# Attention with the value matmuls in halves between the score halves, probability sums that alternate between two partial sums over the first eight key tiles, and denominators in four pieces instead of seven

## What is computed

```
q, k, v = x @ Wq.T, x @ Wk.T, x @ Wv.T            # split in 16 heads of 32
attn    = softmax(q @ k.T / sqrt(32))              # over 2048 keys, per head
x       = layernorm(x + attn @ v)
y       = (x @ sign(W).T) * scale + bias, clipped to +-100
out     = layernorm(x + y)
```

## Time and profile before

| what | value |
|---|---|
| median of 3 runs | 2724.6 us (2723.04 to 2725.27) |
| span of the profiled execution | 2721.4 us |
| around it: median less that span | 3.2 us (the execution's own time is not shown apart) |
| PE, ACT, DVE, POOL busy | 2686.9, 2261.1, 2308.4, 341.1 us |
| exponentials, first to last start | 549.9 to 2426.3 us |
| granted TensorE clock, mean | 0.994 |

### The profile page before, as it was taken

The page is one execution under the profiler, slowest core; times in us unless marked ns, Lnnn a source line. Parts: engine busy times, 40 slices in busy tenths (PEclk is TensorE's granted clock), DMA queues, the critical chain, the costliest instruction groups (busy, mean ns, idle before and its releaser), DMA issues.

```text
span 2721.4 us, 76294 instructions
## 1 busy us (share of the span) xinstructions
PE 2686.9 (99%) x32088; PEld 1351.0 (50%) x32088; DVE 2308.4 (85%) x1983; ACT 2261.1 (83%) x2726; POOL 341.1 (13%) x342
## 2 busy tenths in 40 slices
PE   9999999999999999999999999999999999979998
PEld 8888888733333333333333333333333333337887
DVE  7444444389999999999999999999999999978998
ACT  5333333399999999999999999999999999965665
POOL 1000000000000000010000000000000000005665
PEclk9999999999999999999999999999999999989999
DMA  6555555557686777768677686867768677655553
GB/s 227 191 194 193 188 186 186 197 132 169 132 176 140 155 157 158 162 126 184 138 153 165 142 172 135 167 147 157 168 131 172 141 159 158 150 145 177 189 189 136
DMA packets 216706, 445.22 MB, mean 164 GB/s; under 512 B 15570, under 2 KB 130258, under 8 KB 189780
## 3 DMA queue, kind: packets, MB, share of 16 engines
q0 software_dynamic: 27504, 200.29, 37.4%
q1 hardware_dynamic: 179108, 222.61, 26.2%
q10 hardware_dynamic: 9792, 17.83, 1.7%
HBM read 122.43 MB, written 117.96 MB: 88 GB/s over the span
## 4 chain that ended last, share of the span: by engine, by line
ACT 48%; PE 31%; issue 16%; DMA 3%; DVE 2%; SPq 0%; DVEq 0%; POOL 0%; ACTq 0%; POOLq 0%
ACT probs L769 48%; PE banks L226 19%; PE banks L1007 7%; DMA total<-partial 2%; PE banks L632 1%; PE banks L996 1%; PE banks L661 1%; PE banks L989 1%; PE banks L1003 1%; DVE partial L818 1%; DVE total L821 0%; DVE partial L821 0%; PE banks L248 0%; PE banks L990 0%; PE banks L254 0%
## 5 line engine op out<-in xcount | busy, mean ns | idle before, releaser
L769 ACT ACTIVATE probs<-banks 128x1024 f32<-128x1024 f32 x2048 | 1877.7, 1457 | 3.9 <-PE banks L632 3.9
L632 PE MATMUL banks<-score_rows 97*32 97x512 f16 x16384 | 1117.4, 380 | 4.5 <-issue 4.0
L661 PE MATMUL banks<-probs,v_keys 128*32 128x512 f32 x8192 | 1060.5, 592 | 0.1
L821 DVE TENSOR_TENSOR partial<-partial,probs 128x2048 f32<-128x2048 f32 x384 | 879.4, 2290 | 33.4
L632 PEld LDWEIGHTS banks<-score_rows 97*32 97x32 f16 x16384 | 361.3, 95 | 708.2 <-ACT probs L769 484.3
L818 DVE TENSOR_TENSOR partial<-probs 128x2048 f32<-128x2048 f32 x192 | 439.6, 2290 | 23.6 <-ACT probs L769 16.7
L601 POOL DMA_DIRECT2D total<-partial x191 | 164.7, 862 | 1713.7 <-DMA total<-partial 703.3
L661 PEld LDWEIGHTS banks<-probs,v_keys 128*32 128x32 f32 x8192 | 249.0, 111 | 209.9 <-ACT probs L769 0.2
L821 DVE TENSOR_TENSOR total<-total,probs 128x2048 f32<-128x2048 f32 x128 | 292.6, 2286 | 6.8
L354 DVE TENSOR_TENSOR qk_lo<-banks,qk_hi 128x512 f16<-128x512 f32 x128 | 88.3, 690 | 241.6 <-ACT qk_hi L309 241.6
L680 PEld LDWEIGHTS banks<-total,ones 128*32 128x32 f32 x3584 | 105.6, 109 | 280.7 <-issue 265.1
(11 more groups left out here) (95 smaller groups left out, 2117.5 us busy)
## 6 DMA issues: line engine op xcount, KB each, us to landing
total<-partial POOLq DMA_DIRECT2D x191, 1024.0 KB, 8.3
scratch_q_raw<-qk_raw SPq DMA_DIRECT2D x16, 1024.0 KB, 5.7
scratch_k_raw<-qk_raw SPq DMA_DIRECT2D x16, 1024.0 KB, 5.7
scratch_v<-v_out SPq DMA_DIRECT2D x16, 1024.0 KB, 5.1
score_rows<-scratch_q_hi SPq DMA_DIRECT2D x128, 128.0 KB, 4.6
score_rows<-scratch_k_hi SPq DMA_DIRECT2D x128, 128.0 KB, 3.5
v_keys<-scratch_v SPq DMA_DIRECT2D x64, 256.0 KB, 5.8
scratch_attn<-wf_scaled SPq DMA_DIRECT2D x64, 256.0 KB
```

Source lines behind the costliest of these rows:

```text
L632: last = nc.tensor.matmul(scores_of(phase, unit)[part, i, :], k_rows[:, h, keys], q_rows[:, h, qb * BLK:(qb + 1) * BLK], start=True, stop= ...
L661: last = nc.tensor.matmul(banks[rows, out_bank(qb), :], v_keys[:, kt, rows], probs[:, kt % P_RING, h, :], start=(kt == 0), stop=(kt == KT ...
L769: nc.scalar.activation(probs[:, kt % P_RING, heads, :], scores_of(it % SLOTS, qb * UNITS + u), ACT.Exp, scale=SCALE / GAIN ** 2).then_inc( ...
L821: nc.vector.tensor_tensor(into, into, probs[:, kt % P_RING], ALU.add).then_inc(a_sum, 1)
```

## The change

Three things are changed, all in `attend`.

1. The step of a key tile is cut in two on TensorE: first score half, first half of the values, second score half, second half of the values. A half of the values is columns 0 to 255 or 256 to 511 of the queries for all four heads, so each value matmul has 256 columns and there are twice as many. The waits of the values stand before the first half, the release of `a_pv` behind the second.
2. The sums take the tiles in another order of groups. Tiles 0 to 7 go alternately to group 0 and group 1 (`GROUP_OF = (0, 1) * PER + ...`), tiles 8 to 11 and 12 to 15 to groups 2 and 3 as before. The first add of group 0 is now that of tiles 0 and 2, the first of group 1 that of tiles 1 and 3. `TAKEN` counts for each tile how many tiles from the start are summed without a hole, and `a_sum` goes by it.
3. The denominators are cut in four pieces of 128 columns, behind tiles 8, 10, 12 and 14.

```diff
+GROUP_OF = (0, 1) * PER + (2,) * PER + (3,) * PER
+PREVIOUS = tuple(max((e for e in range(kt) if GROUP_OF[e] == GROUP_OF[kt]), default=None) for kt in range(KT))
+def taken_after(kt):
+    used = {e for k in range(kt + 1) if PREVIOUS[k] is not None for e in (PREVIOUS[k], k)}
+    return next(e for e in range(KT + 1) if e not in used)
+TAKEN = tuple(taken_after(kt) for kt in range(KT))
-DEN_TILES = tuple(range(8, 15))
-DEN_EDGES = (0, 80, 152, 224, 296, 368, 440, BLK)
+DEN_TILES = (8, 10, 12, 14)
+DEN_EDGES = (0, 128, 256, 384, BLK)
...
-        def values(it, qb, kt):
+        def values(it, qb, kt, part):
+            cols = slice(part * BLK // 2, (part + 1) * BLK // 2)
...
-                last = nc.tensor.matmul(banks[rows, out_bank(qb), :], v_keys[:, kt, rows], probs[:, kt % P_RING, h, :],
-                                        start=(kt == 0), stop=(kt == KT - 1))
-            last.then_inc(a_pv, 1)
+                last = nc.tensor.matmul(banks[rows, out_bank(qb), cols], v_keys[:, kt, rows], probs[:, kt % P_RING, h, cols],
+                                        start=(kt == 0 and part == 0), stop=(kt == KT - 1), skip_group_check=True)
+            if part == 1:
+                last.then_inc(a_pv, 1)
...
-                if kt + LAG < KT:
-                    scores(it, phase, qb, kt + LAG)
...
-                values(it, qb, kt)
+                for half in range(2):
+                    if kt + LAG < KT:
+                        scores(it, phase, qb, kt + LAG, (half,))
...
+                    values(it, qb, kt, half)
...
-                    g, place = divmod(kt, PER)
-                    if place == 0:
+                    g, before = GROUP_OF[kt], PREVIOUS[kt]
+                    if before is None:
                         continue
...
-                        nc.vector.tensor_tensor(into, probs[:, (kt - 1) % P_RING], probs[:, kt % P_RING], ALU.add).then_inc(a_sum, 2)
+                        nc.vector.tensor_tensor(into, probs[:, before % P_RING], probs[:, kt % P_RING],
+                                                ALU.add).then_inc(a_sum, TAKEN[kt] - TAKEN[kt - 1])
                     else:
-                        dve.wait_ge(a_sum, st * KT + kt + P_RING)
+                        dve.wait_ge(a_sum, st * KT + TAKEN[before] + P_RING)
```

More of the change, by code:

```diff
@@ L616, in _, with fast_scores @@
         pe.sem_inc(a_merged, GROUPS - 1)
-        def fast_scores(it, phase, qb, kt):
-            if kt == 0:
+        def fast_scores(it, phase, qb, kt, halves=(0, 1)):
+            if kt == 0 and halves[0] == 0:
                 pe.wait_ge(a_q[qb], it * FIRST_Q + FIRST_Q)
-            if qb == 0 and kt % TPB == 0:
+            if qb == 0 and kt % TPB == 0 and halves[0] == 0:
                 pe.wait_ge(a_k[kt // TPB], it * FIRST_K + FIRST_K)
-            for half in range(2):
+            for half in halves:
                 unit = qb * UNITS + 2 * kt + half
@@ L634, in fast_scores, with exact_scores @@
                 last.then_inc(a_score, 1)
-        def exact_scores(it, phase, qb, kt):
+        def exact_scores(it, phase, qb, kt, halves=(0, 1)):
             st = it * QB + qb
-            if kt == 0:
+            if kt == 0 and halves[0] == 0:
                 pe.wait_ge(m_q, st * 32 + 32)
-            if kt % TPB == 0:
+            if kt % TPB == 0 and halves[0] == 0:
                 pe.wait_ge(m_k[kt // TPB % 2], (st * QB // 2 + kt // TPB // 2) * 16 + 16)
             keys = slice(kt % (2 * TPB) * P, (kt % (2 * TPB) + 1) * P)
-            for half in range(2):
+            for half in halves:
                 unit = qb * UNITS + 2 * kt + half
@@ L650, in exact_scores @@
                 last.then_inc(a_score, 1)
-        def values(it, qb, kt):
+        def values(it, qb, kt, part):
             st = it * QB + qb
[L654 to L658, removed]
+            cols = slice(part * BLK // 2, (part + 1) * BLK // 2)
+            if part == 0:
+                if qb == 0 and kt % TPB == 0:
+                    pe.wait_ge(a_v[kt // TPB], it * 16 + 16)
+                pe.wait_ge(a_prob, st * UNITS + 2 * kt + 2 + SLOTS)
+                if kt == 0:
+                    pe.wait_ge(a_dout, st + 1)
             for h in range(G):
                 rows = slice(HD * h, HD * h + HD)
-                last = nc.tensor.matmul(banks[rows, out_bank(qb), :], v_keys[:, kt, rows], probs[:, kt % P_RING, h, :],
-                                        start=(kt == 0), stop=(kt == KT - 1))
-            last.then_inc(a_pv, 1)
+                last = nc.tensor.matmul(banks[rows, out_bank(qb), cols], v_keys[:, kt, rows], probs[:, kt % P_RING, h, cols],
+                                        start=(kt == 0 and part == 0), stop=(kt == KT - 1), skip_group_check=True)
+            if part == 1:
+                last.then_inc(a_pv, 1)
         def denominators(it, qb, piece):
@@ L686, in steps @@
             for kt in tiles:
-                if kt + LAG < KT:
-                    scores(it, phase, qb, kt + LAG)
[L689 to L692, removed]
-                values(it, qb, kt)
+                for half in range(2):
+                    if kt + LAG < KT:
+                        scores(it, phase, qb, kt + LAG, (half,))
+                    elif qb < QB - 1:
+                        scores(it, phase, qb + 1, kt + LAG - KT, (half,))
+                    elif it is not LAST:
+                        scores(it + 1, phase + 1, 0, kt + LAG - KT, (half,))
+                    values(it, qb, kt, half)
                 if kt in DEN_TILES and qb > 0:
@@ L812, in item @@
                     dve.wait_ge(a_prob, st * UNITS + 2 * kt + 2 + SLOTS)
-                    if place == 1:
+                    if PREVIOUS[before] is None:
                         if g == 0:
@@ L817, in item @@
                             dve.wait_ge(a_merged, st * (GROUPS - 1) + g)
[L818 to L821 removed]
+                        nc.vector.tensor_tensor(into, probs[:, before % P_RING], probs[:, kt % P_RING],
+                                                ALU.add).then_inc(a_sum, TAKEN[kt] - TAKEN[kt - 1])
+                    else:
+                        dve.wait_ge(a_sum, st * KT + TAKEN[before] + P_RING)
+                        nc.vector.tensor_tensor(into, into, probs[:, kt % P_RING], ALU.add).then_inc(a_sum, TAKEN[kt] - TAKEN[kt - 1])
                     if kt == OUT_AFTER and not (first and qb == 0):
```

## The result

| | before | after |
|---|---|---|
| median, both kernels on one chip | 2723.82 us (2722.43 to 2725.27, 4 runs) | 2745.56 us (2743.46 to 2750.73, 4 runs) |
| span of the profiled execution | 2721.4 us | 2742.5 us |
| first and last start of an exponential | 549.9, 2426.3 us | 549.9, 2447.9 us |

The ratio is 1.0081, with a 95% interval of 1.0068 to 1.0094. The forecast was slower, at 2735 us, with 2725 to 2744 as the range. The direction was right; the loss is 21.7 us instead of 10.2, and the median lies outside the range. From here on "late piece" means a first denominator piece that waits for the merges and comes later than TensorE's own pace.

What follows compares the result with a forecast made beforehand. ScalarE's exponentials, 0.917 us each, were taken to bound attention. Late merges 8.8, late blocks 0.5, last block 1.2, less 0.3 gained, make 10.2 us; with 2721.4 + 3.2 that gives 2735 us, range 2725 to 2744.

Steps and rivals of the forecast that it cites:

- What bounds the kernel: Attention: ScalarE's exponentials set the pace at 0.917 us each; TensorE's small deficit is covered, merges just fit their room.
- Part 1: Order of the sums: every block's first merge is issued 1.18 us later, VectorE idling about 1.1 us before tile 2.
- The room of 28.4 us: Time from first merge issue to TensorE's stop at the next block's first piece: 29.7 - 1.18 - 0.08, exceeded in 15 blocks.
- Part 2: Denominators in four pieces: the wider first piece takes 0.08 us off the cover; 0.5 us in all for late blocks.
- Part 3: Values in halves on TensorE: nothing to 0.02 us a tile more, 1.75 against ScalarE's 1.834, with a more even supply.
- the rival that TensorE can't be fed: Attention: if issue is limited to 29 ns an instruction, blocks need 31.5 us, 136 us more, 2860 us; chance 0.06.
- The signs: Expected in the profile: weight loads waiting over 25 us for merges, VectorE idle about 1 us, ScalarE gaps in fifteen blocks.
- late pieces in attention: Merge chains longer than their room in 15 of 63 blocks, by 1.2 us at most, stop TensorE and ScalarE: 8.8 us.
- last exponential to the last denominators: End of the last block, which waits outright on its merges: the first merge's delay is paid in full, 1.2 us.
- gains of even supply: Score halves spaced evenly in attention win back part of ScalarE's 3.9 us idle time: 0.3 us.
- The rival of no change: Chains shorten by half a microsecond, or the cover, the lateness overlapping exponentials absorb, exceeds 0.46 us: 2725 to 2730; chance 0.27.
- The faster one: TensorE's write bursts held ScalarE back in attention; even supply frees 16 us: 2709, or 2719 with late merges; chance 0.05.

Runs made afterwards that it cites:

- e1: Kernel before with only the alternating order of the sums, values whole and seven denominator pieces kept: 8.1 us more than before, ratio 1.0026.
- e3: Kernel before with only the four denominator pieces behind tiles 8, 10, 12 and 14: -0.45 us against before, ratio 0.9996.
- e9: Kernel before with values in quarters of 128 columns, all behind the score halves: 346.8 us more than before, ratio 1.1272.
- e2: Kernel before with only the values in halves between the score halves, sums and pieces kept: 19.1 us more than before, ratio 1.0067.
- e8: Changed kernel with the sums in the old order, so halves and four pieces without the alternation: 9.9 us more than before, ratio 1.0036.
- e11: Kernel before with each block's first merge also waiting for tile 11's first exponential, issued at 20.75 instead of 18.04 us: 28.7 us more, ratio 1.0105.

## Why the prediction failed, step by step

**What bounds the kernel: right.** ScalarE set the pace before and after; outside the stops and the lower clock the ends of its exponentials lie 0.917 us apart in both (medians). Their starts don't tell the pace as well: most of them lie 0.905 us apart in both kernels, a record growing by the difference, until a late score takes the overlap back.

**Part 1, the first merge 1.18 us later: right in mechanism and size.** Measured are 1.07 us (19.11 against 18.04 us behind the end of the block's first exponential, medians over the blocks), and VectorE waited for ScalarE before the first sum for 79.7 us in 64 blocks, 1.25 each, forecast as 1.1. The room of 28.4 us priced this part, with the chains of before, at 8.8 us, and at 10.0 with the last block; e1, which does only this, costs 8.1. That this is so close is in part luck: e1's chains were shorter than before's (26.3 against 26.5 us), and with them the same formula gives 5 to 6 us, where the exponentials of the profiled execution took 7.9 us longer.

**Part 2, four pieces: right.** Nothing by e3; the 0.5 us put down for it don't show.

**Part 3, the step that failed.** The text says: "I take nothing to 0.02 us a tile; TensorE stays at 1.75 against 1.834", and of the rival that TensorE can't be fed: "Against it: the 16 instructions of a small piece are through in 0.12 us". Both statements are true of a short stretch, and e9 shows how true: even 64 value instructions a tile don't slow the stretch. (The rival's 2.1 x 64 is 134, not 136; nothing hangs on it.) The halves alone, in e2, cost 19.1 us, and on top of the alternation, together with the four pieces that alone do nothing, 13.6 (21.7 less 8.1), where the text put them at nothing. The error was to test a supply by a burst. The rival, for its part, supposed a steady rate limit of 29 ns an instruction, which would have cost 136 us; 27 ns an instruction was in fact sustained for most of the time. What there is lies between the two: now and then, it seems, the next 16 KB of program come late. By itself that would have cost little here: five stops, 1.0 us, and one in a piece. But the same kernel's merges take longer, 26.9 us instead of 26.5 and up to 31.0 instead of 29.6. That was the assumption hidden in "In 15 of the 63 blocks the chain is longer": it used the chains of before. So the term that was mis-sized is the excess of the merges over their room: with the measured chains the same formula gives 15 to 17 us in 14 to 16 blocks (the more when each block's own issue time is taken) instead of 8.8 in 15.

**The clock, missing from the sum.** The text has each excess stop TensorE and then ScalarE "for as long". Behind three of the late pieces the granted clock was 0.50, and that cost 5 to 6 us more.

**The signs.** The weight loads' wait for merges (39.0 us, "over 25") and VectorE's idle time (1.25 us) came as forecast. ScalarE's gaps didn't: there are 20 besides the one ahead of the first exponential, up to 2.6 us long, where about fifteen of 0.3 to 1.2 were named. The last piece came 0.9 us later, not over 1.

| term, us | forecast | measured |
|---|---|---|
| late pieces in attention | 8.8 | about 16 (15 to 17 by the formula with the measured chains) |
| lower clock behind them | not named | 5 to 6 |
| four pieces | 0.5 | none (e3) |
| last exponential to the last denominators | 1.2 | 0.9 |
| gains of even supply | -0.3 | none |
| sum | 10.2 | 21.6 + 0.9 between the profiled executions up to there |

The first measured line is the 21.6 us by which the last exponential starts later, less the two that follow; its split is worked out from single stretches and holds to a microsecond or two. The last term is read between the start of the last exponential and the first piece behind it: 2426.3 to 2432.82 before, 2447.9 to 2455.34 after. The unchanged last stage is 1.4 us shorter in this execution, so that the spans differ by 21.1.

The parts don't add up, which fits one shared room. e1 (8.1) and e8 (9.9) make 18.0 together; both in one kernel make 21.7. A chain that just fits costs nothing, and every further tenth of a microsecond costs in more blocks. e2 costs more than e8, which has four pieces instead of seven, so 48 instructions a block less, and 10 stops instead of 22. So the four pieces help the halves, though alone they do nothing.

**What stays open.** Why more program makes the merges slower. The packets share the DMA engines with the merges, and the means rise with the instructions (832: 26.2 and 26.6; 880: 26.3 to 26.5, and 26.0 in e11; 1088: 26.9, 26.9 and 27.1; 1136: 27.2 and 27.3; 1648: 28.0). But the queue of instructions has only 0.7% of the engines' time after and 0.6% before, and no run takes the packets away with all else equal. Why one packet is late and the next isn't, is open as well.

The rival of no change (0.27) named a larger cover; none was seen. The faster one (0.05) wanted exponentials closer than 0.917 us; by their ends there are none that last, and by their starts (0.905) they are no closer after than before.

## What to carry to other kernels

When instructions are split or added, work out not only their time on the engine but what they add to the program that has to be brought in, and look at the queue of the instructions and for idle time marked "issue" in the middle of a run; a burst that goes fast proves nothing about the supply. A wait that just fits (29.6 us of DMA in 29.7 of room) is not free but the next thing to break: give it a tile of slack before anything beside it is moved. And when a forecast uses the measured lengths of a DMA chain, put in that the change may lengthen them: the loss grows faster than the delay.

## What the runs showed of the hardware

- Packets of 16 KB, one for some 256 instructions of TensorE, come all through the run: 246 packets before, 297 after, 438 in e9. The Trainium skill, page "Trainium Architecture — The Big Picture", section "The software stack", has the instruction streams brought into each engine's memory at load; this trace shows packets on that queue during the whole execution, and stops that end 1.2 to 1.8 us behind one.
- The number of stops rises steeply with the instructions of a block of 29.33 us: 832 and 880 give none in seven kernels, 1088 give 5 to 10, 1136 give 18 and 22, 1648 give 138.
- Matmuls with 128 columns on 32 columns of the array, each with its own weights, follow each other every 27 to 29 ns with a granted clock of 1.00 (e9: 30 of them and two more from 1003.53 to 1004.41), those with 256 columns every 54 ns.
- After TensorE had stood idle for 3.2, 2.6 and 2.1 us at a piece, the granted clock was 0.50 for 3.4, 6.8 and 3.4 us, beginning between 0.6 us before its restart and 1.0 behind it. After two other such stops of 2.1 and 2.3 us it stayed at 1.00. At that level it makes a tile in 3.4 us, and ScalarE, which bounds the stage, is no longer the bound.
- Merges issued later in the block are faster: by 0.5 us a chain on the mean at 2.7 us later (e11), and there by 1.1 us in every fourth block, where the chains are longest. What they then stand beside on the DMA engines wasn't separated.
